# A sort that begins with a small first part, and layer ends without padding tiles and without edge counts

## The chip, the cores and the metric

The kernel runs on one core of a Trainium2 chip. The metric is the device time of one execution in microseconds (us), the median of several runs. A measurement of this kernel can tell about 0.2% (8 us) from no change.

## The reference, cut to what matters

There are 3125 nodes with 128 features and 103,125 directed edges (sorted by `dst`), each with one of nine types. `edge_index` is `[src, dst]`, so the sums of the first part run over `src`: the edges come in the wrong order for them.

```
# three layers (l = 0, 1, 2), 9 weight matrices 128x128 and 9 biases each
X = einsum('ne,ref->rnf', out, weights[l])
msg = X[edge_type, dst] + biases[l][edge_type]
hidden = segment_sum(msg, src, num_segments=N);  relu except after the last
x = layernorm(x + hidden)
# attention over the same edges
alpha = cos(x[row], x[col]) * beta, softmax over each row's edges
out = segment_sum(alpha * x[col], row)
x = layernorm(x + out)
```

## The kernel before, in words

The kernel has four stages.

**The sort (0 to 526 us).** The edges lie in SBUF as 128 rows of 808 columns. They have to be put in the order of their `src` group (31 groups of `RB` = 102 nodes, one more for padding: `NK` = 32 buckets). VectorE (DVE) makes the group number of each edge, then for each bucket a 0/1 map over all 808 columns (`eq`, L425). TensorE (PE) counts these maps (two products of 404 columns per bucket, L1067). From the counts DVE works out bucket totals (`counts`; PE spreads them, L1071), and the place of each bucket's first edge on each row (`bases`, L458). It also packs each edge into one word (`word`, L460 to L467). Then `place(lo, n, first)` works through all 32 buckets for `n` columns: PE makes the place of each edge by two products into one of two PSUM banks (`bucket`, L1078 and L1079), and DVE takes the maximum over buckets (L475, L479). The first `CP` = 332 columns are placed first; GpSimd (POOL) then scatters them, one indirect DMA per column, into a table in DRAM (L1036), which SyncE's queue (SP) loads back (L905). The other `EP` = 476 columns are placed next; they are not scattered but put in order by products of one-hot matrices on PE (L1148, 476 x 4), which end in PSUM. Both results are added; PE and DVE make the list of gathers from it (`rows`), which releases POOL's gathers.

Beside it PE makes layer 0's products x times weights (`first_x`, 75 steps of a bias product L1097 and a product L1099; each is copied by ScalarE (ACT), and stored by SP). Sixteen of them stand between the buckets of the 476 columns, one after every second bucket; the other 59 follow, and the one-hot products L1148 come behind all of them. The bias is split into three bf16 parts by POOL (L1021 to L1030), on 96 rows x 1152 columns, and POOL also writes the selection matrices (`choose`, L1015).

**Three layers (526 to 3619 us).** Each layer has `GT` = 806 gathers, one tile of 128 edges each, by POOL (L1054), into a ring of `GR` = 62 slots. PE multiplies each gathered tile by a one-hot matrix (`use_tiles`, L1193, four tiles to a PSUM bank), DVE adds the result to the group's sum (`take_tiles`, L665) and makes later one-hots (`one_hot`, L594). As a tile can belong to two groups, and to round up to turns of `BODY` = 24, a layer has `NT` = 840 tile places in 35 turns (`TURNS`); the gathers end at place 836 at the latest. Turns 0 to 83 of all 105 turns also count edges between nodes: 10 steps per turn with five 128x510 products each (L1202), whose one-hots DVE makes (L599, L600), and which ACT evicts at each group's end. Blocks 0 to 19 of the next layer's products x times weights are made early, inside the layer, and are stored by SP. At the layer's end the last six groups are turned (`turn_sums`, L1226), DVE takes the relu (L675), blocks 20 to 24 are made (L1237, DVE adds the bias, L689) and stored by five DMAs (L912); POOL's first gather of the next layer waits for these stores. Blocks 0 to 19 are then made again without stores, unless one came too early, and the next layer's tiles follow.

**The attention (3619 to 3999 us)** works on dense 128x384 blocks. The change doesn't touch it.

Of the kernel before, what the change touches and what calls it, by code (L numbers as in the profile page):

```python
# [47 lines left out]
def gnn_program(nc, x, src, dst, edge_type, weights, biases, beta, out):  # L48
# [32 lines left out]
    CP = 332  # L81
    EP = ET - CP
# [33 lines left out]
    AT_TURN = [-(-(REACH[k] * NT // MB + BODY) // BODY) for k in range(EARLY)]  # L116
    PAIR_BANKS, ALL_BANKS = (6, 7), (5, 6, 7)
    EARLY_STORES, ALL_STORES = EARLY + 1, 2 * EARLY + 1
# [14 lines left out]
    assert (L - 1) * TURNS < CTURNS < L * TURNS and CB % CR == 0 and CQ + CR < KW  # L133
# [23 lines left out]
    counts = nc.dram_tensor("edge_counts", (NB, P, NP), F32, kind="Internal").ap()  # L157
    absent = nc.dram_tensor("edge_absent", (NB, P, NP), BF16, kind="Internal").ap()

    with ExitStack() as ctx:  # L160
# [63 lines left out]
        bias_d = part(RF)  # L224
        bias_x = [part(RF // 2, BF16) for _ in range(3)]
# [20 lines left out]
        bias_t, ones_3 = bias[:, 0:RF // 2].bitcast(BF16), bias[:, RF // 2:RF // 2 + P // 2].bitcast(BF16)  # L246
# [47 lines left out]
        s_bias = sem("s_bias")  # L294
        s_eq = sem("s_eq")
# [60 lines left out]
        UNITS, CONSTANTS, BIAS_PARTS = 15, 21, 33  # L356
# [36 lines left out]
        def _(dve):  # L393
# [19 lines left out]
            nc_.memset(zerob[:, :], 0.0)  # L413
# [10 lines left out]
            for b in range(NK):  # L424
                nc_.tensor_scalar(eq[:, b, :], keyb, float(b), None, ALU.is_equal).then_inc(s_eq, 1)  # L425

# [33 lines left out]
            step(nc_.tensor_scalar(posi, posi, float(MB - 1), -float(RB), ALU.min, ALU.mult))  # L460
            step(nc_.tensor_tensor(posi, srci, posi, ALU.add))

            step(nc_.scalar_tensor_tensor(out=word, in0=dsti, scalar=float(R), in1=typei,
                                          op0=ALU.mult, op1=ALU.add))
            step(nc_.scalar_tensor_tensor(out=word, in0=posi, scalar=float(1 << ROW_BIT), in1=word,
                                          op0=ALU.mult, op1=ALU.add))
            step(nc_.tensor_scalar(word, word, 1.0, None, ALU.add))  # L467

# [15 lines left out]

            place(0, CP, 0)
            ti, tj = (t.bitcast(I32)[:, 0:CP] for t in tmps[0:2])
# [158 lines left out]
            for q in range(CR - 1):  # L645
                cell_hots(q)

            def take_tiles(l, i, cells):
                first = NT * l
                for u in range(BODY):  # L650
                    n, t = divmod(u, SLOTS)
                    if t == 0:
# [792 lines left out]
```

## Time and profile before

| | |
|---|---|
| median of 3 runs | 3996.73 us (3995.7 to 3997.86) |
| the profiled execution: its time, its span | 4001.13 us, 3999.4 us |
| busy: PE, DVE, POOL, ACT | 73%, 68%, 66%, 20% |
| POOL gathers: layers 1 and 2, layer 0 | 1612 and 806, 945 and 948 ns each |
| TensorE's granted clock, mean | 0.847 |

The profile shows one execution. A busy share is an average over four stages with different limits, so the stages are read one by one: the chain of waits tells which engine's work ends last, the timeline of each engine shows when its instructions start, how long they take and what ended the idle time before them, and the table by windows gives the granted clock of TensorE (1.00 is 2.4 GHz, 0.50 is 1.2 GHz).

### The profile page before, as it was taken

Reading aid. Unit: us, or ns where it says so; the run is one execution under the profiler, and the core shown is the slowest. Engines: PE = TensorE matmul, PEld = TensorE weight load, DVE = VectorE, ACT = ScalarE, POOL = GpSimd, SP = SyncE. Lnnn points to the kernel's source line nnn. Section 1 sums busy time; section 2 is a strip of 40 time slices with the busy share of each in tenths; the row PEclk is TensorE's granted clock in tenths of the full one; section 3 lists DMA queues with packets and bytes.
Section 4 is the critical chain, followed back from the end, with each engine's and each line's share of the span. In section 5 each row is a group of like instructions: output and inputs, shape, how many; then the busy total and the mean of one; then the engine's idle time right before and its main releaser. Section 6 shows DMA issues by size and latency. Waiting matters only on the chain.

```text
span 3999.4 us, 57212 instructions
## 1 busy us (share of the span) xinstructions
PE 2913.7 (73%) x14372; PEld 1860.7 (47%) x14372; DVE 2714.3 (68%) x9164; ACT 801.6 (20%) x1939; POOL 2632.2 (66%) x2787
## 2 busy tenths in 40 slices
PE   6999966676777678777777777787774444447998
PEld 2555544444444445444444444554443333335776
DVE  6488875676667668776767665777664333337999
ACT  0688801000100010100100010001000000004665
POOL 4777767777777775777777777577777777770000
PEclk6999988898889989998899888999885555557999
DMA  2300012342433332333343333323333111113554
GB/s 83 135 2 2 2 42 73 88 108 73 107 88 103 73 108 83 80 85 103 83 106 79 103 86 79 115 73 75 87 78 73 53 53 53 53 53 115 193 190 135
DMA packets 374776, 337.04 MB, mean 84 GB/s; under 512 B 262929, under 2 KB 326985, under 8 KB 374342
## 3 DMA queue, kind: packets, MB, share of 16 engines
q0 software_dynamic: 88000, 158.81, 16.4%
q1 hardware_dynamic: 83110, 113.84, 8.3%
q10 hardware_dynamic: 203360, 60.73, 6.2%
q8 instruction: 141, 2.31, 0.2%
q14 instruction: 165, 1.35, 0.1%
HBM read 226.02 MB, written 130.74 MB: 89 GB/s over the span
## 4 chain that ended last, share of the span: by engine, by line
POOL 46%; PE 26%; issue 17%; DVE 7%; DMA 3%; ACT 1%; SPq 0%; DVEq 0%; POOLq 0%; ACTq 0%
POOL region L1054 46%; PE ps L1148 9%; PE ps L1193 3%; PE ps L1276 3%; PE ps L1202 3%; PE ps L1237 3%; DMA region<-x_of_type_in_layer,arrays 2%; PE ps L1304 2%; PE ps L1099 1%; DVE region L792 1%; DVE region L665 1%; DVE region L599 1%; PE ps L1279 1%; DVE region L600 1%; PE ps L1079 1%
## 5 line engine op out<-in xcount | busy, mean ns | idle before, releaser
L1054 POOL DMA_INDIRECT region<-x_of_type_in_layer,arrays x1612 | 1523.3, 945 | 552.3 <-issue 477.9
L1193 PE MATMUL ps<-region,oh 128*102 x5040 | 1112.6, 324 | 789.9 <-SPq L918 490.4
L1193 PEld LDWEIGHTS ps<-region,oh 128*102 128x102 f32 x5040 | 920.9, 204 | 1340.6 <-issue 1078.6
L1202 PE MATMUL ps<-region 128*128 128x510 f16 x4200 | 1355.0, 410 | 182.6 <-ACT ps L1362 138.7
L594 DVE TENSOR_SCALAR oh<-iota_w,arrays 128x102 f32<-128x102 f32 x2528 | 730.1, 290 | 1051.6 <-PE ps L1193 1026.3
L1054 POOL DMA_INDIRECT region<-x_of_type,arrays x806 | 763.7, 948 | 265.5 <-issue 263.0
L665 DVE TENSOR_TENSOR region<-region,ps 102x128 f32 x2520 | 713.9, 283 | 3.1 <-issue 2.8
L1202 PEld LDWEIGHTS ps<-region 128*128 128x128 f16 x4200 | 433.6, 104 | 249.5 <-issue 197.8
L1373 ACT COPY region<-ps 128x510 f32<-128x510 f32 x155 | 89.8, 579 | 2246.4 <-PE ps L1202 2245.9
L599 DVE TENSOR_SCALAR region<-ps,arrays 128x640 f16<-128x640 f16 x844 | 459.6, 545 | 0.0
L1036 POOL DMA_INDIRECT scattered_edges<-region x332 | 322.4, 971 | 155.6 <-issue 106.3
L600 DVE TENSOR_SCALAR region<-ps,arrays 128x510 f16<-128x510 f16 x844 | 400.0, 474 | 0.0
L1148 PE MATMUL ps<-region 128*128 128x420 f16 x1904 | 340.6, 340 | 0.0
L1343 ACT ACTIVATE region<-region 128x128 f16<-128x128 f16 x952 | 291.8, 389 | 44.2 <-DVE region L572 43.9
L1148 PEld LDWEIGHTS ps<-region 128*128 128x128 f16 x1904 | 184.8, 97 | 156.1 <-issue 0.9
L573 DVE TENSOR_SCALAR region<-region 128x840 f16<-128x840 f16 x476 | 248.0, 521 | 0.0
L1237 PE MATMUL ps<-wsb,hB 128*128 128x384 f32 x540 | 210.5, 544 | 9.0 <-DVE hB L675 8.8
L689 DVE TENSOR_TENSOR region<-ps,bias 128x384 f32<-128x384 f32 x270 | 148.7, 551 | 64.6 <-PE ps L1237 61.9
L1304 PEld LDWEIGHTS ps<-nodes,region 128*128 128x128 f32 (+1 forms) x1250 | 163.8, 191 | 53.9 <-DVE region L792 28.5
L1304 PE MATMUL ps<-nodes,region 128*128 128x129 f32 (+1 forms) x1250 | 181.3, 282 | 7.2 <-DVE region L792 7.0
L572 DVE TENSOR_SCALAR region<-region 128x128 f16<-128x128 f16 x476 | 121.8, 256 | 82.3 <-PE ps L1148 82.1
L1276 PE MATMUL ps<-hB,region 128*128 128x384 f32 (+1 forms) x450 | 170.8, 461 | 0.0
(243 smaller groups left out, 1621.3 us busy)
## 6 DMA issues: line engine op xcount, KB each, us to landing
x_of_type_in_layer<-region SPq DMA_DIRECT2D x90, 576.0 KB
edge_counts<-region ACTq DMA_DIRECT2D x155, 255.0 KB
arrays<-edge_counts SPq DMA_DIRECT2D x40, 960.0 KB, 5.0
region<-x_of_type_in_layer,arrays POOLq DMA_INDIRECT x1612, 2.5
edge_absent<-region ACTq DMA_DIRECT2D x155, 127.5 KB
region<-edge_absent SPq DMA_DIRECT2D x40, 480.0 KB, 3.8
region<-x_of_type,arrays POOLq DMA_INDIRECT x806, 2.5
x_of_type<-x0st SPq DMA_DIRECT2D x51, 192.0 KB, 1.9
```

The costliest lines, as they stand in the source:

```text
L594: ins = nc_.tensor_scalar(oh[:, t % U, 0:RB], iota_r, rowf[:, t % NT:t % NT + 1], None, ALU.is_equal)
L599: nc_.tensor_scalar(cl[:, q % CR, :], lane_h, key1[:, q:q + 1], None, ALU.is_equal)
L600: nc_.tensor_scalar(cr[:, q % CR, :], lane_h[:, 0:CW], key2[:, q:q + 1], None, ALU.is_equal).then_inc(s_co, 1)
L665: nc_.tensor_tensor(h, h, ps[0:RB, 6 + n % 2, t * D:(t + 1) * D], ALU.add).then_inc(s_add, 1)
L1036: pool.indirect_dma_start(out=table, out_offset=bass.IndirectOffsetOnAxis(ap=pay[:, t, 1:2], axis=0), in_=pay[:, t, 0:1], in_offset=None). ...
L1054: pool.indirect_dma_start(out=grow[:, t % GR * D:(t % GR + 1) * D], out_offset=None, in_=xts[l], in_offset=bass.IndirectOffsetOnAxis(ap=gi ...
L1148: mm = pe.matmul(ps[:, 2 * d + n, 0:HW], oh_q[:, k, d, :], oh_s[:, k, n * HW:(n + 1) * HW], start=False, stop=False, skip_group_check=True)
L1193: mm = pe.matmul(ps[0:RB, 6 + n % 2, t * D:(t + 1) * D], oh[:, u % U, 0:RB], grow[:, bass.ds(at[u % PAIRS], D)], start=True, stop=True)
L1202: mm = pe.matmul(ps[:, c, 0:CW], cl[:, q % CR, c * P:(c + 1) * P], cr[:, q % CR, :], start=False, stop=False, skip_group_check=True)
L1237: pe.matmul(ps[:, banks[j % len(banks)], 0:G3], hB[:, b * P:(b + 1) * P], wsb[:, l * R + 3 * c:l * R + 3 * c + 3, :].rearrange("p r d -> p ...
L1304: mm = pe.matmul(ps[0:w, 4 + c % 2, t * VW:(t + 1) * VW], ring[:, b % RING, t * P:t * P + w], nodes[:, j, :], start=False, stop=(j == NB - ...
L1343: ins = act.activation(oh_q[:, k, d, :], hot_q[:, k, :], ACT.Copy, scale=cols[:, 4 * t + 2 + d:4 * t + 3 + d])
```

## The change

It has two parts. All times of day stay out here; the numbers are sizes.

**The sort.**
- A first part of `CA` = 64 columns is placed, and written out as `first_cells`, before the other 268 of the 332 (`cells`); POOL starts its scatters at `first_cells` and waits for `cells` at column 64. The buckets are worked through three times (64, 268, 476 columns).
- The packing of `word` moves from behind `bases` to behind the maps `eq`, ahead of the counts. The list of group ends (`late` to `past`) moves behind the last `place`.
- Of the 75 `first_x` steps, eight come before the buckets (two ahead of the totals' product, six behind it), one after every second bucket of the 268 and of the 476 columns (16 + 16), and 35 after.
- The bias is split by POOL on 9 rows x 128 columns (five short instructions in place of thirteen), goes to DRAM in three parts, and comes back as 3 rows x 1152. The other layers' biases are loaded behind it.
- `choose` is written by ACT, not by POOL.
- PE begins with 24 products of zeros (`WARM`), 512 columns each.
- POOL waits for layer 0's stores before it waits for `rows`.

**The layer ends.**
- Tile places 836 to 839 are left out in each layer (`LAST_USE`); the semaphores are advanced by as much.
- The last turn of each layer, and the first turn of layers 1 and 2, count no edges (`QUIET`); the 84 counting turns are now the others, 0 to 87.
- The first eight one-hots of a layer are made behind the products of blocks 20 to 24, not in the last turn of the layer before.
- Block 24 is stored in three pieces (`PIECES`).

```diff
@@ sort, DVE
             for b in range(NK):
                 nc_.tensor_scalar(eq[:, b, :], keyb, float(b), None, ALU.is_equal).then_inc(s_eq, 1)
+            step(nc_.tensor_scalar(posi, posi, float(MB - 1), -float(RB), ALU.min, ALU.mult))
...
+            step(nc_.tensor_scalar(word, word, 1.0, None, ALU.add))
...
-            place(0, CP, 0)
...
+            place(0, CA, 0)
+            cells(0, CA, "first_cells")
+            place(CA, CP - CA, NK)
+            cells(CA, CP, "cells")
+            place(CP, EP, 2 * NK)
...
-            place(CP, EP, NK)
             dve.wait_ge(s_fill, 16)
+            dve.wait_ge(s_later, 32)
@@ sort, POOL
-            finished(nc_.tensor_copy(choose[0:2 * NK, :, :],
-                                     chosen[0:2 * NK, :].unsqueeze(2).to_broadcast([2 * NK, NK, P])))
...
-            H3 = 3 * NK
-            finished(nc_.tensor_copy(bias_x[0][0:H3, :], bias[0:H3, 0:RF]))
...
+            finished(nc_.tensor_copy(bias_x[0][0:R, :], bias_s[0:R, :]))
...
-            pool.wait_ge(s_d, marks["cells"])
+            pool.wait_ge(s_d, marks["first_cells"])
             for t in range(CP):
+                if t == CA:
+                    pool.wait_ge(s_d, marks["cells"])
@@ sort, PE
+            pe.wait_ge(s_d, marks["zeros"])
+            for n in range(WARM):
+                pe.matmul(ps[:, 7, :], zerob[:, 0:P], zerob[:, :], start=True, stop=True)
...
+            pe.wait_ge(s_const, 64)
+            turn_nodes(0)
+            pe.wait_ge(s_parts, 64)
+            for q in range(2):
+                first_x(q)
+            pe.wait_ge(s_d, marks["counts"])
+            pe.matmul(ps[:, 0, 0:NK], ones[0:NK, :], tot_diag[0:NK, :], start=True, stop=True).then_inc(s_t, 1)
+            for q in range(2, FIRST_X):
+                first_x(q)
+            pe.wait_ge(s_d, marks["bases"])
+            pe.wait_ge(s_pool, CONSTANTS)
+            pe.wait_ge(s_choose, 1)
             for b in range(NK):
-                bucket(0, CP, b, b)
...
+                bucket(0, CA, b, b)
             for b in range(NK):
-                bucket(CP, EP, b, NK + b)
+                bucket(CA, CP - CA, b, NK + b)
                 if b % 2:
-                    first_x(b // 2)
-            for q in range(NK // 2, NB * XC):
+                    first_x(FIRST_X + b // 2)
+            for b in range(NK):
+                bucket(CP, EP, b, 2 * NK + b)
+                if b % 2:
+                    first_x(FIRST_X + NK // 2 + b // 2)
+            for q in range(FIRST_X + NK, NB * XC):
                 first_x(q)
@@ sort, SP
-            sp.dma_start(bias[:, :], biases.rearrange("l r f -> (l r f)").partition_broadcast(P)).then_inc(s_bias, 16)
+            sp.dma_start(bias_s[0:R, :], biases[0]).then_inc(s_bias, 16)
...
+            sp.wait_ge(s_pool, BIAS_PARTS)
+            for n in range(3):
+                sp.dma_start(bias_parts[n].rearrange("(r d) -> r d", r=R), bias_x[n][0:R, :]).then_inc(s_parts, 16)
+            sp.wait_ge(s_parts, 48)
+            sp.dma_start(bias_t, bias_parts).then_inc(s_parts, 16)
@@ layers
+    QUIET = {TURNS * l + i for l in range(L) for i in (0, TURNS - 1)} - {0}
+    CELLS_IN = [n for n in range(L * TURNS) if n not in QUIET]
+    LAST_USE = NT - SLOTS
...
+                for u in range(min(BODY, LAST_USE - i * BODY)):
...
-                    one_hot(first + i * BODY + u + U)
+                    if i * BODY + u + U < NT:
+                        one_hot(first + i * BODY + u + U)
...
                     take_made(l, LATE_BLOCKS, ALL_BANKS)
+                    for u in range(U):
+                        one_hot(NT * l + u)
...
+                types = R // PIECES[b]
+                for lo in range(0, R, types):
```

How the instructions stand, on the engines that wait or are waited for. PE at the program's start, before:

```order
L1060 UNCONDITIONAL_BRANCH
L1067 MATMUL ps<-region 64x404 x64
L1071 MATMUL ps<-region,ones 128x32
L1078 MATMUL ps<-region 128x332
L1079 MATMUL ps<-region 128x332
```

PE at the program's start, now (L1094 are the products of zeros, L1099 the counts, L1114 the transposes of the nodes, L1125 and L1127 a `first_x` step, L1137 the totals):

```order
L1089 UNCONDITIONAL_BRANCH
L1094 MATMUL ps<-zerob 128x512 x24
L1099 MATMUL ps<-region 64x404 x64
L1114 MATMUL ps<-ident,nodes 128x128 x8
L1125 MATMUL ps<-bias 128x384
L1127 MATMUL ps<-wsb,hB 128x384
L1125 MATMUL ps<-bias 128x384
L1127 MATMUL ps<-wsb,hB 128x384
L1137 MATMUL ps<-region,ones 128x32
```

Two `first_x` steps and the transposes for them stand ahead of the totals' product; six more steps follow it, and then the buckets of 64 columns.

DVE from `bases` (L458) to the end of the first `place`, before (L460 to L467 pack the words, L475 and L479 take the maximum over buckets):

```order
L458 CAST region<-region 64x808
L460 TENSOR_SCALAR arrays<-arrays 128x808
L461 ISA arrays<-arrays 128x1616
L463 SCALAR_TENSOR_TENSOR arrays<-arrays 128x808
L465 SCALAR_TENSOR_TENSOR arrays<-arrays 128x808
L467 TENSOR_SCALAR arrays<-arrays 128x808
L475 COPY arrays<-ps 128x332 x2
L479 TENSOR_TENSOR arrays<-arrays,ps 128x332 x30
L481 TENSOR_TENSOR arrays<-arrays 128x332
```

DVE from `bases` (L482) to `first_cells` (L505), now:

```order
L482 CAST region<-region 64x808
L490 COPY arrays<-ps 128x64 x2
L494 TENSOR_TENSOR arrays<-arrays,ps 128x64 x30
L496 TENSOR_TENSOR arrays<-arrays 128x64
L497 TENSOR_SCALAR arrays<-arrays 128x64
L502 TENSOR_SCALAR arrays<-arrays 128x64
L503 TENSOR_SCALAR arrays<-arrays 128x64
L504 COPY region<-arrays 128x64
L505 SCALAR_TENSOR_TENSOR region<-arrays 128x64
L490 COPY arrays<-ps 128x268 x2
```

The packing is gone from here, and the first part is 64 columns wide and complete before the 268 begin.

PE at the end of layer 0, before (L1193 a tile, L1202 counts of edges, L1226 `turn_sums`, L1237 `make_x`):

```order
L1193 ISA
L1193 MATMUL ps<-region,oh 102x128
L1202 MATMUL ps<-region 128x510 x2
L1193 ISA
L1193 MATMUL ps<-region,oh 102x128
L1202 MATMUL ps<-region 128x510 x2
L1226 MATMUL ps<-ident,region 128x102 x6
L1237 MATMUL ps<-wsb,hB 128x384 x15
L1226 MATMUL ps<-ident,region 128x102 x25
```

PE at the end of layer 0, now (L1234 a tile, L1267 `turn_sums`, L1278 `make_x`):

```order
L1234 ISA
L1234 MATMUL ps<-region,oh 102x128
L1234 ISA
L1234 MATMUL ps<-region,oh 102x128
L1267 MATMUL ps<-ident,region 128x102 x6
L1278 MATMUL ps<-wsb,hB 128x384 x15
L1267 MATMUL ps<-ident,region 128x102 x25
```

The counts of edges between the tiles are gone from this turn, and it is four tiles shorter.

## Rows read from the trace of the kernel before

**Rows 1.** The page, part 4: shares of the chain that ended last, by line.
```profile
POOL region L1054 46%; PE ps L1148 9%; PE ps L1193 3%; PE ps L1276 3%; PE ps L1202 3%; PE ps L1237 3%; DMA region<-x_of_type_in_layer,arrays 2%; PE ps L1304 2%; PE ps L1099 1%; DVE region L792 1%; DVE region L665 1%; DVE region L599 1%; PE ps L1279 1%; DVE region L600 1%; PE ps L1079 1%
```

**Rows 2.** Windows: length; busy (count) PE, PEld, DVE, ACT, POOL; clock, DMA.
```profile
16.00:19.00 3.00, 1.88 (x8) 0.71 (x6) 3.00 (x2) 0.00 (x0) 2.94 (x2) 1.00 0.97 258
...
28.00:31.00 3.00, 3.00 (x12) 1.63 (x11) 3.00 (x11) 0.00 (x0) 0.08 (x1) 0.61 0.00 0
...
90.00:95.00 5.00, 5.00 (x15) 1.58 (x15) 2.33 (x5) 0.96 (x2) 3.78 (x5) 0.82 0.14 46
```

**Rows 3.** Timeline of DVE in the sort: start, us, instruction [idle before, releaser].
```profile
13.10 19.40 DVE L425 TENSOR_SCALAR region<-arrays 128x808 bf16<-128x808 bf16 x32
35.74 0.57 DVE L431 COPY region<-ps 64x404 f32<-64x404 f32 x1 [3.25 <-PE ps L1067]
...
45.11 0.58 DVE L460 TENSOR_SCALAR arrays<-arrays 128x808 int32<-128x808 int32 x1
...
49.44 0.91 DVE L475 COPY arrays<-ps 128x332 f32<-128x332 f32 x2
...
52.45 0.50 DVE L479 TENSOR_TENSOR arrays<-arrays,ps 128x332 f32<-128x332 f32 x1 [0.28 <-PE ps L1079]
...
75.94 0.50 DVE L490 SCALAR_TENSOR_TENSOR region<-arrays 128x332 int32<-128x332 int32 x1
...
84.83 0.65 DVE L479 TENSOR_TENSOR arrays<-arrays,ps 128x476 f32<-128x476 f32 x1 [1.97 <-PE ps L1079]
85.85 0.65 DVE L479 TENSOR_TENSOR arrays<-arrays,ps 128x476 f32<-128x476 f32 x1 [0.37 <-PE ps L1079]
...
96.10 1.26 DVE L479 TENSOR_TENSOR arrays<-arrays,ps 128x476 f32<-128x476 f32 x2 [0.77 <-PE ps L1079]
```

**Rows 4.** Timeline of PE in the sort: a product of `first_x`.
```profile
120.41 0.81 PE L1099 MATMUL ps<-wsb,hB 128*128 128x384 f32 x2
```

**Rows 5.** Timeline of POOL in the sort: its first scatter.
```profile
77.36 1.22 POOL L1036 DMA_INDIRECT scattered_edges<-region  x1 [49.28 <-DVE shiftcol L496]
```

**Rows 6.** Timeline of SP's queue: the load of the scattered table.
```profile
507.27 0.32 SPq L905 DMA_DIRECT2D arrays<-scattered_edges  x1
```

**Rows 7.** Chain that ended last, in order of time: start, us, what.
```profile
166.22 1.67 PE ps L1119 x4
...
172.69 340.36 PE ps L1148 x1904
...
524.41 0.50 POOLq L362
```

**Rows 8.** Timeline of PE at the ends of layer 0 and layer 2.
```profile
1537.23 0.46 PE L1193 MATMUL ps<-region,oh 128*102 x2 [2.11 <-SPq L918]
...
1545.57 1.03 PE L1226 MATMUL ps<-ident,region 102*128 102x102 f32 x6 [2.90 <-DVE region L665]
...
3613.01 3.73 PE L1193 MATMUL ps<-region,oh 128*102 x16 [3.30 <-SPq L918]
3618.75 5.50 PE L1226 MATMUL ps<-ident,region 102*128 102x102 f32 x31 [2.01 <-issue]
```

**Rows 9.** Timeline of DVE at layer 0's end: the last bias sums.
```profile
1558.68 1.78 DVE L689 TENSOR_TENSOR region<-ps,bias 128x384 f32<-128x384 f32 x3 [0.16 <-PE ps L1237]
```

**Rows 10.** Timeline of POOL at the layer ends, and 62 gathers later.
```profile
1534.25 0.96 POOL L1054 DMA_INDIRECT region<-x_of_type,arrays  x1 [0.30 <-issue]
1564.01 0.94 POOL L1054 DMA_INDIRECT region<-x_of_type_in_layer,arrays  x1 [28.80 <-DMA x_of_type_in_layer<-region]
...
1641.16 0.94 POOL L1054 DMA_INDIRECT region<-x_of_type_in_layer,arrays  x1 [2.54 <-PE ps L1193]
...
2678.18 0.94 POOL L1054 DMA_INDIRECT region<-x_of_type_in_layer,arrays  x1 [1.80 <-PE ps L1193]
```

**Rows 11.** The page, part 6: a DMA of 192 KB, us to landing.
```profile
x_of_type<-x0st SPq DMA_DIRECT2D x51, 192.0 KB, 1.9
```

**Rows 12.** Windows at layer 0's end, columns as in rows 2.
```profile
1552.00:1553.00 1.00, 1.00 (x4) 0.56 (x3) 0.21 (x2) 0.00 (x0) 0.00 (x0) 0.65 0.15 65
```

More of the change, by code:

```diff
@@ L223, in gnn_program @@
         twice, chosen, tot_diag = part(NK), part(NK), part(NK)
-        bias_d = part(RF)
-        bias_x = [part(RF // 2, BF16) for _ in range(3)]
+        bias_s, bias_d = part(D), part(D)
+        bias_x = [part(D // 2, BF16) for _ in range(3)]
         used[0] = MB * D
@@ L412, in _ @@
             step(nc_.memset(typei[:, REST:ET], 0), "cleared")
-            nc_.memset(zerob[:, :], 0.0)
+            step(nc_.memset(zerob[:, :], 0.0), "zeros")
             nc_.memset(nodes[:, :, D:VW], 1.0)
@@ L646, in _, with take_tiles @@
                 cell_hots(q)
-            def take_tiles(l, i, cells):
-                first = NT * l
-                for u in range(BODY):
+            def take_tiles(l, i):
+                first, cells = NT * l, CELLS_IN.get(TURNS * l + i)
+                for u in range(min(BODY, LAST_USE - i * BODY)):
                     n, t = divmod(u, SLOTS)
@@ L1069, in _ @@
             mm.then_inc(s_t, 1)
-            pe.wait_ge(s_d, marks["counts"])
-            pe.matmul(ps[:, 0, 0:NK], ones[0:NK, :], tot_diag[0:NK, :], start=True, stop=True).then_inc(s_t, 1)
             def bucket(lo, n, b, k):
-                if b == 0:
-                    pe.wait_ge(s_d, marks["bases"])
                 if k >= 2:
@@ L1179, in _, with use_tiles @@
                       skip_group_check=True)
-            def use_tiles(l, i, cells):
-                first = NT * l
-                for u in range(BODY):
+            def use_tiles(l, i):
+                first, cells = NT * l, CELLS_IN.get(TURNS * l + i)
+                for u in range(min(BODY, LAST_USE - i * BODY)):
                     n, t = divmod(u, SLOTS)
@@ L1186, in use_tiles @@
                         at, due = steps_at((i * BODY + u) // PAIRS)
-                    if cells and u == 0:
-                        ready = banks_at(TURNS * l + i)
+                    if cells is not None and u == 0:
+                        ready = banks_at(cells)
                     if t == 0:
@@ L1195, in use_tiles @@
                     if t == SLOTS - 1:
-                        mm.then_inc(s_used, 1)
-                    for q, c in PARTS[u] if cells else ():
-                        k = i * CB + (CB * TURNS * l + q)
+                        mm.then_inc(s_used, 1 if i * BODY + u < LAST_USE - 1 else 1 + (NT - LAST_USE) // SLOTS)
+                    for q, c in PARTS[u] if cells is not None else ():
+                        k = cells * CB + q
                         if c == 0:
@@ L1256, in _ @@
                         pe.wait_ge(s_xe, made[0])
[L1257 removed]
+                    use_tiles(l, i)
             pe.wait_ge(s_cz, CG + CG * MB)
@@ L1326, in copy_turned @@
                 act.copy(hB[:, 4 * c * P:(4 * c + n) * P], ps[:, 2 + c % 2, 0:n * P]).then_inc(s_x0c, 1)
+            act.wait_ge(s_pool, CONSTANTS - 2)
+            act.copy(choose[0:2 * NK, :, :],
+                     chosen[0:2 * NK, :].unsqueeze(2).to_broadcast([2 * NK, NK, P])).then_inc(s_choose, 1)
             copy_turned(0)
```

115 lines of the change are left out of this document (60 added, 55 removed).

## The prediction

> **What bounds the kernel now.** I read the chain of waits first: POOL's gathers hold 46% of it, PE's one-hot products of the sort 9% [rows 1]. Layer by layer the gathers follow each other without gaps, apart from the stretch between two layers (28.8 us of idle time at the first [rows 10]) and one stall 62 gathers later. So three stretches are worth something: the sort ahead of the first gather, the ends of the layers, and these stalls. Work that PE or DVE loses inside a layer is worth nothing, since POOL's 806 gathers end it.
>
> In the sort two paths meet. POOL's scatters start at 77.36 [rows 5] and end in SP's load at 507.27 [rows 6]. PE's 1904 one-hot products start at 172.69 and end at 172.69 + 340.36 = 513.05 [rows 7]. The load needs about 1.9 us (a smaller one does [rows 11]), so POOL's path has up to 513.05 - 507.27 - 1.9 = 3.9 us of slack. Both paths must get shorter, or nothing is won.
>
> **The sort, as far as the first scatter.** The 32 maps `eq` take DVE 19.4 us, from 13.10 to 32.50 [rows 3]. Their pace is not even: 2 instructions touch the window 16 to 19, in which POOL is busy for 2.94 us with splitting the bias, and 11 the window 28 to 31, in which POOL is idle [rows 2]. I read 0.28 us for one without POOL. The change leaves POOL five instructions on 128 columns, on a bias that lands early, and gives `choose` to ACT; so I take 32 x 0.28 = 9.0 us, and the maps end at 22.1. (The Trainium skill, "SBUF — State Buffer", section "Who interferes with whom", says that VectorE in a 2-port mode and GpSimd lock a shared port pair, and that the later one fully blocks. The rows agree; without that lock the maps would stay at 32.5, which is a rival below.)
>
> Now the packing of words follows, which stood between 45.11 and the first COPY at 49.44 [rows 3], 4.3 us: 26.4. PE's 64 products for the counts must be done too: 12 of them touch the window 28 to 31 at a clock of 0.61 [rows 2], 0.25 us each, and by the clock 0.15 at 1.00. From the first map at 13.4 on that ends between 23.2 and 29.4. I take 27.0 for the first copy of the counts, before 35.74 [rows 3]. The 24 products of zeros matter only here, for 0 to 3 us. (The Trainium skill, "TensorE: Matmul & The Clock Gate", section "What's actually happening", has the slow clock as the state at rest. The row of 16 to 19 shows 1.00 before any long activity [rows 2], so here the trace differs. By the page the counts would start slowly without the zeros; by the row they start fast anyway. The sum goes by the 27.0.)
>
> From there to `bases` nothing changes: 45.11 - 35.74 = 9.4 us, 36.4. Meanwhile PE has eight `first_x` steps at 0.81 [rows 4], 6.5 us, in two gaps that are idle now; if they ran at the slow clock (about 1.55, below) they would delay `bases` or the buckets by up to 4 us. SP gets two new waits here: for POOL's split, and for the parts in DRAM. Behind them stand the load of the parts (which PE's first step needs), the other biases, and the fill of the table (which POOL's first scatter needs). The loads kept the DMA engines busy at 16 to 19 and had drained by 28 to 31 [rows 2]; now the first of them is 9 rows in place of 128, so the two trips to DRAM, 1.9 us each [rows 11], end before PE asks for the parts near 28. I cost this at nothing; if the loads drain no earlier, the totals, and with them everything, come up to 4 us later.
>
> The first part then has 32 buckets of 64 columns. A bucket of 332 columns took 0.50 + 0.28 = 0.78 us [rows 3]. For 64 columns this is the upper end, 0.25 (a DVE instruction that short) the lower. What is left is the way from PE to DVE and back, over two banks; I take 0.36, near the lower end. 36.4 + 0.4 + 32 x 0.36 + 1.3 for six short instructions = 49.6, before 75.94 + 0.50 = 76.44 [rows 3]. **POOL's scatters start 26.8 us earlier**, at 50.5, if the 0.9 us from the mark to the start stay [rows 3, 5]. The second 268 columns are wanted 64 scatters (about 80 us) later and are ready by then.
>
> **The sort, PE's path.** From 48.2 on PE has 16 pairs of buckets (268 columns) with a `first_x` each, 16 pairs of 476 columns, 35 more `first_x`, and the close. The price depends on the clock. A pair of 476 with its step took 0.65 + 1.97 + 0.65 + 0.37 = 3.64 us at 0.5, and 1.26 + 0.77 = 2.03 at 1.00 [rows 3]; in between the clock rose at about 91.8 [rows 2], some 15 us after pairs and steps had begun. At the fast clock the buckets of a pair are 2.03 - 0.81 = 1.22; with 268 columns between 0.69 (by width) and 1.22, and I take 0.9: 1.7 for the pair with its step. At the slow clock a bucket of 332 is 0.78, of 268 about 0.67, and a step 3.64 - 2 x 1.05 = 1.55: 2.9 for the pair. The buckets of 64 leave PE mostly idle, so I expect the slow clock at 48.2 and, as before, a rise after some 15 us: 5 pairs x 2.9 + 11 x 1.7 = 33.2, to 81.4. Then 16 x 2.03 = 32.5, to 113.9; 35 x 0.81 and some transposes = 29.3, to 143.2; the close as before, 172.69 - 166.22 = 6.5 [rows 7], to 149.7. **PE's path is 23.0 us shorter.** DVE's list of group ends, now behind the last `place` (3 us), lies beside the 35 steps; POOL's path, 26.8 shorter and with slack, is not the bound. POOL also does its load of a value (0.50 [rows 7]) and six waits ahead of `rows`: 0 to 1.3 us, I put 0.5.
>
> **The layer ends.** After the last gather PE had eight tiles with counts of edges, from 1537.23 until DVE's sums let it turn them at 1545.57: 8.3 us [rows 8]. Now it has four tiles without counts. Layer 2's end shows tiles without counts: eight took 3.73, and 3618.75 - 3613.01 - 3.73 = 2.0 more went by for DVE's sums and one-hots [rows 8]. Four tiles: 2.0, and 1.0 for four sums without one-hots. Gain 8.3 - 3.0 = 5.3 (4.3 if the 2.0 stay, 6.3 if the clock is high). The last store: from the last bias sum at 1558.68 + 1.78 = 1560.46 to POOL at 1564.01 were 3.55 us [rows 9, 10]; with a last piece of 192 KB 1.9 [rows 11] + 0.9 = 2.8: 0.8 less (0 to 1.6). The eight one-hots stand behind all of this. 6.1 per boundary, 12.2 for both.
>
> The stalls at 1641.16 and 2678.18 were ended by PE's tiles [rows 10]: 2.54 + 1.80, less the usual 0.30 each, 3.7 us. The first turn without counts gives PE and DVE 24 tiles' worth of lead before the ring is full, more than the 1.7 us that the moved one-hots take, so I take the whole 3.7 (0 if the turns behind it fall back). At the end of layer 2 four tiles fewer give 5.7 - 3.0 = 2.7.
>
> **Sum.** 23.0 + 0.5 + 12.2 + 3.7 + 2.7 = 42.1 us. The profiled execution took 4001.1: 3959.0; it lies 4.4 above the median of the runs, so 3954.6, say **3955**.
>
> **The rivals.**
> - *POOL becomes the sort's bound.* If the clock rises soon after 48.2, the first pairs cost 16 x 1.7 = 27 and PE gains 29; POOL's path allows 26.8 + 3.9. For it: at layer 0's end the clock rose faster, some 7 us after PE began to turn the sums at 1545.57 [rows 8, 12]. 6 us more: 3949. Chance 0.20.
> - *The clock stays low through the 268 columns.* 16 x 2.9 = 46.4, then 4 pairs x 3.64 + 12 x 2.03 = 39: PE's products start near 169, the sort gains 3.3, in all 22: 3974. For it: before, the whole first `place` went at 0.78 a bucket, that is at the slow clock, and nothing raised it. Chance 0.15.
> - *The maps don't get faster* (the change doesn't do what I read into it, the slow ones being DVE's own): maps and words end at 36.8, everything is 9.8 later, 3965. Against it: the two windows [rows 2]. Chance 0.05.
> - *The layer ends give it back*: the turn without counts lets the clock fall, and the 15 products between layers run longer at 1.55 in place of 0.81. They already start slow (0.65 in the window in which it rises [rows 12]); some 5 us lost at each boundary, and the stalls stay: 3966. Chance 0.08.
> - *Slower:* the clock stays low until the `first_x` are done. Then 46.4 + 16 x 3.64 + 35 x 1.55 + 0.9 + 6.5 = 166 from 48.2 on: the products start at 214, 42 us later than now, and the other gains of 19 leave 22 us lost: 4019. It decides itself at about 157 us: a clock that rises before that leaves the kernel no slower. Against it: it rose at 92 in the same mix. Chance 0.05, of which a good half ends within 0.2% of before or near it.
>
> **How the numbers follow.** The forecast has 0.47. The range 3944 to 3975 takes in the quick clock with two or three us more at the ends, and the late clock; what it leaves out is the slow case and part of the tails. 0.2% is 8 us, about what a measurement of this kernel can tell: faster 0.95, same 0.03, slower 0.02.
>
> **What would show it.** Right: `eq` at 0.28 each; the first scatter near 50; the one-hot products starting near 150 with the load of the table landed before they end; gaps of about 24 us between layers; no POOL stall 62 gathers into layers 1 and 2. Wrong: a granted clock of 0.5 well past 75, a wait of PE for the bias parts ahead of the totals, or a first scatter later than 56.

## The result

The changed kernel is **slower**: a median of 4035.42 us against 3997.59 us before, 20 executions each. The ratio with its 95% interval, 1.0077 (1.0064 to 1.0089), leaves out as slow runs the four executions that lie over 1.5% above the fastest one; the ratio of the medians is 1.0095. The forecast was 3955 with a range of 3944 to 3975. The profiled execution took 4035.99 us with a span of 4034.2 us, 34.8 us more than the 3999.4 before. One of the 20 executions took only 3976.61 us, 48 us less than the next; its mean granted clock is 0.858, and that of the other 19 is 0.840 to 0.846. No trace of it was kept. What follows describes the others.

Three rows divide this. The lines of POOL's gathers and PE's one-hot products after (line, engine, operation, count: shortest/median/longest in ns, first and last start in us; forms):

```profile
L1189 PE MATMUL ps<-region x1904: 338/341/559, 223.8 to 564.8; 128*128 128x420 f16 x191
L1083 POOL DMA_INDIRECT region<-x_of_type,arrays x806: 940/944/1428, 577.5 to 1585.7; - x162
L1083 POOL DMA_INDIRECT region<-x_of_type_in_layer,arrays x1612: 940/944/1048, 1610.5 to 3646.6; - x180
```

The one-hot products start at 223.8, before at 172.69 [rows 7], and the first gather at 577.5 where it was 526.2: the sort lost 51.3 us. From the first gather to the last go 3069.1 us, before 3083.7: the layers gained 14.6. Behind the last gather the span needs 387.6 in place of 389.5: another 1.9 gained. 51.3 - 14.6 - 1.9 = 34.8. So the layer ends did what they were to do, and the whole loss lies ahead of the first gather.

**The granted clock tells where.** The table by windows of the kernel after, with the busy time and the number of instructions of each engine, then the granted clock, the DMA share and GB/s:

```profile
20.00:30.00 10.00, 8.26 (x38) 3.99 (x36) 9.59 (x19) 2.03 (x4) 0.00 (x0) 0.94 0.65 206
30.00:40.00 10.00, 10.00 (x17) 3.11 (x16) 3.85 (x15) 2.39 (x5) 0.00 (x0) 0.50 0.27 98
...
90.00:100.00 10.00, 10.00 (x22) 3.44 (x23) 2.60 (x6) 1.43 (x3) 7.56 (x9) 0.50 0.20 65
...
180.00:190.00 10.00, 10.00 (x23) 3.95 (x24) 10.00 (x33) 3.47 (x8) 7.56 (x9) 0.71 0.32 108
190.00:200.00 10.00, 10.00 (x29) 3.59 (x28) 2.77 (x9) 4.34 (x10) 6.54 (x7) 1.00 0.50 169
```

PE is busy for at least 9.9 of the 10 us of every slice from 30 on, and yet it has the 1.2 GHz level until about 185; before, the clock was back at about 92 [rows 2]. It came back 18 us after the last bucket had ended (at 167.5), when only `first_x` steps were left.

**The second thing is the price of a step.** The timeline of PE, once at a clock of 0.50 and, from 200 on, once at 1.00 (start, busy time, line, operation, rows and columns of the two operands):

```profile
150.62 0.49 PE L1125 MATMUL ps<-bias 3*128 3x384 bf16 x1
151.04 1.65 PE L1127 MATMUL ps<-wsb,hB 128*128 128x384 f32 x2
152.48 0.61 PE L1106 MATMUL ps<-region 128*128 128x476 bf16 x1
...
200.59 0.33 PE L1125 MATMUL ps<-bias 3*128 3x384 bf16 x1
200.86 0.91 PE L1127 MATMUL ps<-wsb,hB 128*128 128x384 f32 x2
201.70 0.33 PE L1125 MATMUL ps<-bias 3*128 3x384 bf16 x1
```

At 1.00 a step takes 201.70 - 200.59 = 1.11 us; before it took 0.81 [rows 4]. The operands are the same but for one: the bias product has 3 rows (3x384) where it had 96. The list of the change said so ("3 rows x 1152"), and the working priced only the trip of these rows through DRAM, not the product. At 0.50 a step takes 152.48 - 150.62 = 1.86 within a pair, some 0.3 more than the forecast's 1.55, and 2.01 where only steps are left.

**What the price is** stands in the loads of weights, which have an engine row of their own (PEld). In the kernel before, with 96 rows, they run beside the product ahead:

```profile
121.06 0.35 PEld L1099 LDWEIGHTS ps<-wsb,hB 128*128 128x128 f32 x2 [0.23 <-issue]
121.54 0.10 PEld L1097 LDWEIGHTS ps<-bias 96*128 96x128 bf16 x1
```

There the f32 product starts at 121.22 and the next bias product at 121.86, so that both loads are early. The same stretch of the kernel after:

```profile
200.59 0.09 PEld L1125 LDWEIGHTS ps<-bias 3*128 3x128 bf16 x1 [0.55 <-issue]
200.85 0.30 PEld L1127 LDWEIGHTS ps<-wsb,hB 128*128 128x128 f32 x2 [0.17 <-issue]
201.70 0.09 PEld L1125 LDWEIGHTS ps<-bias 3*128 3x128 bf16 x1 [0.55 <-ACT x0st L1378]
201.96 0.19 PEld L1127 LDWEIGHTS ps<-wsb,hB 128*128 128x128 f32 x1 [0.17 <-issue]
```

Each load starts when its own product does (200.59 beside 200.59, 201.96 0.26 behind the bias product's 201.70): it has not started beside the product ahead. The bias load's 0.09 and the first f32 load's 0.19 are 0.28 of the 0.30 us.

### The profile page after: what moved, and what is told of

It is laid out like the page before. It is cut to its first block, busy times and chain, and to the rows that moved or that the text cites. A ratio compares the mean times of both kernels' runs of the same rounds, so it can differ in the third digit from the quotient of the medians.

```text
span 4034.2 us, 57356 instructions
## 1 busy us (share of the span) xinstructions
PE 2993.4 (74%) x14434; PEld 1869.5 (46%) x14436; DVE 2695.3 (67%) x9182; ACT 803.5 (20%) x1940; POOL 2617.6 (65%) x2780
## 4 chain that ended last, share of the span: by engine, by line
POOL 41%; PE 29%; issue 15%; DVE 9%; DMA 3%; ACT 2%; DVEq 0%; SPq 0%; POOLq 0%; ACTq 0%
POOL region L1083 41%; PE ps L1189 8%; PE ps L1243 4%; PE ps L1234 4%; PE ps L1316 3%; DMA region<-x_of_type_in_layer,arrays 2%; PE ps L1127 2%; PE ps L1344 2%; DVE region L687 2%; DVE region L620 2%; PE ps L1278 2%; DVE region L621 1%; DVE region L816 1%; PE ps L1107 1%; DVE oh L615 1%
## 5 line engine op out<-in xcount | busy, mean ns | idle before, releaser
L1234 PE MATMUL ps<-region,oh 128*102 x5016 | 1102.4, 322 | 779.6 <-SPq L952 477.1
L1234 PEld LDWEIGHTS ps<-region,oh 128*102 128x102 f32 x5016 | 911.1, 202 | 1337.7 <-issue 1078.2
L594 DVE TENSOR_SCALAR region<-region 128x840 f16<-128x840 f16 x476 | 238.6, 501 | 0.0
L1278 PE MATMUL ps<-wsb,hB 128*128 128x384 f32 x540 | 212.5, 548 | 9.4 <-DVE hB L698 8.5
```

Source lines behind the costliest of these rows:

```text
L1234: mm = pe.matmul(ps[0:RB, 6 + n % 2, t * D:(t + 1) * D], oh[:, u % U, 0:RB], grow[:, bass.ds(at[u % PAIRS], D)], start=True, stop=True)
L1278: pe.matmul(ps[:, banks[j % len(banks)], 0:G3], hB[:, b * P:(b + 1) * P], wsb[:, l * R + 3 * c:l * R + 3 * c + 3, :].rearrange("p r d -> p ...
```

## The experiments

**1. The layer ends alone.** The kernel before with the lines marked "layers" of the diff; the sort untouched.

> The kernel before with the layer-end half of the change alone (the quiet first and last turns, the last uses left out, the block that is stored in three pieces); the sort is that of before. First theory, that the two halves are independent and the loss lies in the sort alone: the stretch from the first gather to the last shortens by 14 to 15 us and the end behind the last gather by about 2, as in the changed kernel, so some 16 us less than before: about 3981. Rival, that the layer ends gained only because the sort was late (more of the counts' work had to wait): under 8 us gained, 3990 or more.

Measured 3983.26 us, ratio 0.9961 (0.9946 to 0.9976). POOL's timeline at the first boundary:

```profile
1556.37 0.94 POOL L1068 DMA_INDIRECT region<-x_of_type_in_layer,arrays  x1 [23.22 <-DMA x_of_type_in_layer<-region]
```

The idle time is 23.22 us (28.8 before [rows 10]); the second boundary has 25.70. From the first gather to the last go 3070.3 us, 13.4 less than before, and the end is 2.7 shorter. This half is worth about 16 us by the trace and 14.5 by the medians, with the sort of before as with the changed one, and the rival is out. (The profiled span is 18.3 shorter; 2.2 of that are a first gather that came earlier by itself.)

**2. The row count of the bias product alone, in the order of before.** One line of the kernel before, with 32 and then with 64 rows:

```diff
-                pe.matmul(ps[:, 4 + q % 4, 0:G3], ones_3[0:3 * NK, :], bias_t[0:3 * NK, c * G3:(c + 1) * G3],
+                pe.matmul(ps[:, 4 + q % 4, 0:G3], ones_3[0:NK, :], bias_t[0:NK, c * G3:(c + 1) * G3],
```

> The kernel before with one thing changed: the bias product of each of the 75 steps of the first X runs over 32 rows instead of 96 (it leaves out the two smaller parts of the bias in layer 0, nothing else). First theory, the row count of the bias product is what makes a step dear and also what holds the clock down: a step alone takes about 1.1 us fast and 2.0 slow (0.81 and 1.57 before), the clock, which rose at about 92 in the kernel before, rises only after the 32 pairs of 476 columns, near 150, and PE starts the one-hot products at 212 or later instead of 172.7: 4037 or more. Second theory, the price is real but the clock goes by the order of the work alone: the clock rises at about 92 as before, 75 x 0.29 = 22 us are lost, start near 195, about 4020. Third theory, 32 rows cost nothing more than 96 (three rows were dear for another reason, or the step was dear through its neighbours): the time of before, 3997.

> The kernel before with the bias product on 64 rows instead of 96 (it leaves out the smallest part of the bias in layer 0, nothing else). If any row count of 64 or less that stands next to 128 costs the change: a step alone 1.1 us fast as with 32 rows, the clock late again, 4037 or more. If the price grows with the rows that are missing: about halfway between 96 and 32 rows, 0.95 us fast, 4015 to 4025. If 64 is as free as 96: 3997.

Measured 4048.27 us, ratio 1.0123 (1.0106 to 1.014), with 32 rows, and 4043.65, ratio 1.0114 (1.0097 to 1.0132), with 64: this one line loses more than the whole change. A step alone takes 1.11 us at 1.00 with either, here the 32-row kernel:

```profile
180.59 0.33 PE L1097 MATMUL ps<-bias 32*128 32x384 bf16 x1
...
181.70 0.33 PE L1097 MATMUL ps<-bias 32*128 32x384 bf16 x1
```

So next to 128 rows 3, 32 and 64 cost the same, and 96 cost nothing extra: it is not the number of rows that is paid, but the change from one class to another. Between two products of 64 rows the load is early again. In the 64-row kernel, where the bias product follows a bucket's second product, it lies beside the bucket's product (from 112.07 on) and ahead of its own (at 112.45), and nothing waited for it:

```profile
112.08 0.11 PEld L1097 LDWEIGHTS ps<-bias 64*128 64x128 bf16 x1
```

Three rows behind 64 are a change again. In the changed kernel, also at 0.50, the bias load starts with its own product (at 150.62), and that product starts 0.51 us behind the bucket's 64-row product, where it was 0.38 above; 32 rows behind 64 give the same 0.51:

```profile
150.61 0.10 PEld L1125 LDWEIGHTS ps<-bias 3*128 3x128 bf16 x1 [0.41 <-issue]
```

The rows tried thus fall into three classes: 3 and 32, 64, and 96 and 128.

The clock, too, follows. In the windows of the 32-row kernel it is at 0.50 until 140 although the order of the work is that of before:

```profile
90.00:100.00 10.00, 10.00 (x18) 2.59 (x18) 2.65 (x5) 1.44 (x3) 7.56 (x9) 0.50 0.13 41
...
140.00:150.00 10.00, 10.00 (x29) 3.82 (x28) 10.00 (x34) 4.17 (x10) 7.56 (x9) 0.91 0.40 138
```

The one-hot products start at 211.8 (32 rows) and 215.0 (64). The second theory (195) is out: the narrow first part is not needed for the low clock. (The Trainium skill, "TensorEngine Tiling (Array Packing)", lists in its section "Available Configurations" modes of 128, 64 and 32 rows, and its section "Key Properties" says that changing the mode drains TensorE. The runs agree if a product is taken to run in the smallest mode that holds its rows, which no run shows directly: 64 rows or fewer next to 128 pay, 32 or 3 next to 64 pay, 96 next to 128 do not.)

**3. The changed kernel with 96 rows again.** The three rows of bias stay where they are; 93 rows of zeros, written by DVE while it waits for the edges, go below them.

```diff
-        bias_t, ones_3 = bias[0:3, 0:RF // 2].bitcast(BF16), bias[0:3, RF // 2:RF // 2 + P // 2].bitcast(BF16)
+        bias_t, ones_3 = bias[0:96, 0:RF // 2].bitcast(BF16), bias[0:96, RF // 2:RF // 2 + P // 2].bitcast(BF16)
...
+            step(nc_.memset(bias_t, 0.0), "bias_zero")
...
-            sp.dma_start(bias_t, bias_parts).then_inc(s_parts, 16)
+            sp.wait_ge(s_d, marks["bias_zero"])
+            sp.dma_start(bias_t[0:3, :], bias_parts).then_inc(s_parts, 16)
```

> The changed kernel with the bias product on 96 rows again (the three rows of bias with 93 rows of zeros below them), all else as changed. First theory, the three rows make the steps dear and hold the clock down: a step alone costs 0.81 fast and 1.57 slow again, the clock rises within the part of 268 columns, PE starts the one-hot products near 150 instead of 224: about 3961. Second theory, only the price comes from the rows and the clock stays low until 185 because narrow buckets come first: about 64 x 0.44 + 11 x 0.29 = 31 us come back, start near 193, about 4004. Third theory, the rows are not it at all: start 224, 4035.

Measured **3959.49 us, ratio 0.9896 (0.988 to 0.9913)**: 76 us less than the changed kernel, and faster than before. PE's one-hot products in this kernel, and its windows:

```profile
L1191 PE MATMUL ps<-region x1904: 337/340/559, 150.5 to 490.8; 128*128 128x420 f16 x191
```

```profile
50.00:60.00 10.00, 10.00 (x26) 3.79 (x26) 3.23 (x8) 1.64 (x4) 7.56 (x9) 0.50 0.20 64
60.00:70.00 10.00, 10.00 (x39) 4.57 (x37) 3.84 (x10) 2.97 (x6) 7.56 (x9) 0.84 0.29 97
70.00:80.00 10.00, 10.00 (x43) 4.45 (x42) 5.09 (x13) 2.77 (x7) 7.56 (x9) 1.00 0.35 119
```

They start at 150.5 (the forecast had 149.7), the clock is back at about 63, some 17 us after the pairs of 268 columns began at 46.6 (the forecast had 15 us), and the first scatter starts at 49.1 (50.5). Stage by stage, from the starts of PE's products in the two traces:

| us | as changed, 3 rows | 96 rows |
|---|---|---|
| first bucket of 64 | 39.9 | 35.5 |
| 268 columns, 16 pairs with steps | 51.4 to 104.2 | 46.6 to 81.1 |
| 476 columns, 16 pairs with steps | 104.2 to 167.5 | 81.1 to 113.9 |
| 35 steps | to 216.2 | to 143.8 |
| close, to the first one-hot product | 223.8 | 150.5 |

The difference of 73.3 us is price and clock together. Price: at a clock of 0.50, 32 steps in pairs at 0.3 us each and some 15 outside of them at 0.45, and at 1.00 the other 28 at 0.30: 25 us by this estimate. The other 48 are put down to the clock, as what is left.

**4. The buckets' second product on 96 rows too.** It has 64 rows in both kernels, and in the changed one it stands next to 128 rows 96 times. `choose` and `base_h` get 32 rows of zeros:

```diff
+            nc_.memset(choose[2 * NK:96, :, :], 0.0)
+            nc_.memset(base_h[2 * NK:96, :], 0.0)
...
-                pe.matmul(ps[:, b % 2, 0:n], choose[0:2 * NK, b, :], base_h[0:2 * NK, lo:lo + n],
+                pe.matmul(ps[:, b % 2, 0:n], choose[0:96, b, :], base_h[0:96, lo:lo + n],
```

> The kernel of a_bias96 with the second product of each bucket (the one that adds a bucket's start) on 96 rows too, 32 of them zeros, instead of 64. First theory, any change of row class between neighbouring products costs about 0.1 us and holds the clock down: on top of a_bias96 the 96 buckets save 0.1 us each, 10 us, and the clock comes back sooner: start near 140 or earlier, 3951 or less. Second theory, only three rows are dear and 64 are not: the time of a_bias96 within 3 us.

> The changed kernel with only the second product of each bucket on 96 rows; the bias product keeps its 3 rows. By the price alone 96 x 0.1 = 10 us come back: start near 214, about 4025. If the clock goes by how many row changes a stretch holds, the part of 268 columns keeps the two changes of each step but loses the eight of its buckets, and the clock rises inside it: start 160 to 180, 3970 to 3990. If the clock goes by the 3-row products themselves, it stays low to the end of the buckets: 4025.

With both products on 96 rows: **3948.06 us, ratio 0.9869 (0.9852 to 0.9885)**, the fastest of the study. With the buckets alone, and the bias left on its 3 rows: 3968.42, ratio 0.9927 (0.991 to 0.9944). The price shows at equal clock (1.00) in PE's timeline, first with 64 and then with 96 rows, from one bias product to the next:

```profile
101.19 0.34 PE L1127 MATMUL ps<-bias 96*128 96x384 bf16 x1
...
102.01 0.36 PE L1108 MATMUL ps<-region 128*128 128x476 bf16 x1
102.30 0.37 PE L1109 MATMUL ps<-region 64*128 64x476 f16 x1
102.61 0.37 PE L1108 MATMUL ps<-region 128*128 128x476 bf16 x1
102.91 0.37 PE L1109 MATMUL ps<-region 64*128 64x476 f16 x1
103.22 0.34 PE L1127 MATMUL ps<-bias 96*128 96x384 bf16 x1
```

```profile
80.81 0.32 PE L1129 MATMUL ps<-bias 96*128 96x384 bf16 x1
...
81.61 0.36 PE L1110 MATMUL ps<-region 128*128 128x476 bf16 x1
81.81 0.37 PE L1111 MATMUL ps<-region 96*128 96x476 f16 x1
82.02 0.37 PE L1110 MATMUL ps<-region 128*128 128x476 bf16 x1
82.22 0.36 PE L1111 MATMUL ps<-region 96*128 96x476 f16 x1
82.43 0.32 PE L1129 MATMUL ps<-bias 96*128 96x384 bf16 x1
```

2.03 against 1.62 us: four changes of rows less, 0.10 us each. The products start 0.30 apart with changes and 0.20 without, while the busy time of one reads 0.36 to 0.37 in both: it is the distance of the starts that shows the price, not the duration. And the loads tell why, first with 64 rows, then with 96:

```profile
102.60 0.10 PEld L1108 LDWEIGHTS ps<-region 128*128 128x128 bf16 x1 [0.21 <-issue]
102.91 0.09 PEld L1109 LDWEIGHTS ps<-region 64*128 64x128 f16 x1 [0.21 <-issue]
```

```profile
82.02 0.10 PEld L1111 LDWEIGHTS ps<-region 96*128 96x128 f16 x1
82.22 0.10 PEld L1129 LDWEIGHTS ps<-bias 96*128 96x128 bf16 x1
```

With 64 rows a load starts with its own product (102.91 and 102.91), with 96 one product earlier (82.02 for the product at 82.22). The 0.10 us of a change are the load that nothing hides. My expectation of 0.1 per bucket was half of it, since a bucket has two changes.

With the bias on 3 rows and the buckets on 96, the clock was back near 52 and the products started at 153.3. So the 3-row products do not hold the clock down by themselves: in the order of the changed kernel it came back early without either kind of change, and only with both kinds it stayed away. (In this trace it had been up once already, from about 35.6 to 42.4, beginning among the 3-row steps ahead of the buckets; in the changed kernel's profile the same steps ended at 0.50.) With both on 96 rows PE's products run from 132.3 to 473.1, and POOL's last scatter starts at 475.2, so that POOL's path ends last: DVE waits 4.82 us for the table that SP loads back, and about 5 us of PE's gain are not seen. (The load took 2.86 us; the prediction had taken 1.9 for it from a smaller one.) That is the first rival of the prediction, in a kernel that it was not written for.

**5. Half as many changes, the same products.** The steps of the changed kernel in pairs: two bias products of 3 rows, then two of 128 (the edit is shortened).

```diff
-                pe.matmul(ps[:, 4 + q % 4, 0:G3], ones_3, bias_t[:, c * G3:(c + 1) * G3],
-                          start=True, stop=False)
-                pe.matmul(ps[:, 4 + q % 4, 0:G3], hB[:, b * P:(b + 1) * P], ...
+                for q in steps: pe.matmul(ps[:, 4 + q % 4, 0:G3], ones_3, ...
+                for q in steps: pe.matmul(ps[:, 4 + q % 4, 0:G3], hB[:, b * P:(b + 1) * P], ...
```

> The changed kernel with the steps of the first X in pairs: two bias products of 3 rows, then the two steps of 128 rows, so 38 groups instead of 75 with the same products. If the price hangs on each change of rows, half of it goes: 37 x 0.4 = 15 us, start near 209, 4020, and less if the clock comes back sooner. If every 3-row product is dear by itself, nothing changes: start 224, 4035.

Measured 3979.59 us, ratio 0.995 (0.9932 to 0.9968), 56 us less than the changed kernel, with every product on its old rows. PE's timeline at 1.00 (two bias products, then the two steps of two products each):

```profile
141.66 0.49 PE L1126 MATMUL ps<-bias 3*128 3x384 bf16 x2
...
143.57 0.49 PE L1126 MATMUL ps<-bias 3*128 3x384 bf16 x2
```

143.57 - 141.66 = 1.91 us for two steps, that is 2 x 0.81 + 0.29: one price for two. The price hangs on the change. And the clock was at 1.00 from 60 on, so here as well fewer changes brought it back; that was worth more than the 15 us of price.

**6. The clock raised by force.** The changed kernel with 32 products of 404 columns on 128 rows between the narrow buckets and the 268 columns:

```diff
+            for n in range(NK):
+                pe.matmul(ps[:, 2, 0:HALF_ET], ltri_up[:, :], eq[:, n, 0:HALF_ET], start=True, stop=True)
```

> The changed kernel with 32 products of 404 columns (128 rows, results unused) put on PE between the narrow buckets and the part of 268 columns; nothing is left out. First theory, products that change between 3, 64 and 128 rows hold the clock down: it rises during the dense stretch and falls to 0.50 again in the part of 268 columns, the added products cost up to 32 x 0.34 = 11 us at the slow clock, start of the one-hot products 224 to 235, 4035 to 4046. Rival, the clock was low only because of the wait and the narrow buckets ahead, and stays up once it is up: pairs with a step of about 1.9 and 2.3 us, start near 173, about 3984.

Measured 3983.28 us, ratio 0.9958 (0.9943 to 0.9973): 52 us less than the changed kernel, for 7.6 us of products that nobody reads. The windows:

```profile
40.00:50.00 10.00, 10.00 (x57) 5.76 (x58) 6.20 (x28) 0.00 (x0) 0.00 (x0) 0.50 0.05 20
50.00:60.00 10.00, 10.00 (x42) 4.68 (x42) 2.28 (x10) 0.44 (x1) 6.00 (x6) 0.79 0.02 2
60.00:70.00 10.00, 10.00 (x41) 4.29 (x40) 4.37 (x11) 3.02 (x7) 7.56 (x9) 1.00 0.30 100
...
150.00:160.00 10.00, 10.00 (x28) 3.50 (x27) 0.00 (x0) 4.35 (x10) 7.66 (x8) 1.00 0.51 177
```

**My theory falls in one point here.** I expected the clock to fall back among the row changes; it stayed at 1.00 from 60 to 160, with 3, 64 and 128 rows in turn, and the products started at 173.0, which was the rival's number. So the changes did not pull a fast clock down here. What the runs show is narrower: buckets and steps that start slow and both change rows stayed slow as long as the buckets lasted (three kernels: as changed, and with 32 and 64 rows of bias in the old order), and the clock came back 18, 8 and 6 us behind the last bucket, among the steps alone. In the order of the changed kernel the same work came up within 17 us of the first pair once one kind of change was gone, halved, or preceded by products without changes. And it is a tendency: the one execution of 3976.61 us of the changed kernel is as fast as the kernels in which the clock came back early.

**7. Does it hold in the old order, too?** The edit of experiment 4 in the kernel before, and the same with the layer ends of experiment 1.

> The kernel before with the second product of each bucket on 96 rows instead of 64, nothing else. If a change of rows is dear and keeps a low clock low in any order of the sort: each of the 64 buckets saves its two changes, about 0.2 us, and the clock, low from 41 to 91 in the kernel before, comes back inside the part of 332 columns; the first scatter starts at 60 to 70 instead of 77, PE's one-hot products at 150 to 160 instead of 172.7, and since POOL's scatters would then end last, some 10 to 17 us are gained: 3980 to 3988. If it is dear only together with the narrow buckets: 3997.

> The kernel of h_before_choose96 with the layer-end half of the change on top. The layer ends do not meet the sort, so 16 us less than h_before_choose96: 3964 to 3972. What separates it from ae_both96 (3948) is then what the small first part and the products between the buckets are worth by themselves once no product changes rows: about 20 us.

Measured 3985.58 us, ratio 0.9973 (0.9963 to 0.9982), and 3969.63, ratio 0.9935 (0.9918 to 0.9951). The clock of the first was at 0.85 in 50 to 60, where the kernel before has 0.50; PE's products started at 153.5 in place of 172.7, the first scatter at 66.6 in place of 77.36. (4.6 us of the scatter's 10.8, and some of the products' 19, are not the edit's: PE's counts ended at 27.3 in place of 35.6, at a clock of 1.00 in the window 20 to 30; the 32-row kernel of experiment 2 had its counts as early, and lost all the same.) POOL's last scatter starts at 494.1 and PE's last product at 494.0, so that 19 us of PE's path bring the first gather only 16 forward. The rows cost something in both orders. And h2_ends_choose96 against ae_both96, 3969.63 against 3948.06, is what the changed sort is worth where neither the buckets nor the steps change rows: about 22 us.

## Why the prediction was wrong

**The step that failed** is in "The sort, PE's path", where a step was taken at 0.81 and 1.55 us and a pair of 268 columns at 2.9 and 1.7, all from rows of the kernel before. Those rows had a bias product of 96 rows. With 3 rows a step is 1.11 and 2.01, and the pair of 268 with its step took 3.24 at the slow clock. The sentence after it, "as before, a rise after some 15 us", fell with it: the clock stayed at 0.50 until 185, 134 us after the pairs had begun. With the one line put back to 96 rows, the rest of that paragraph holds: 34.5 us for the 268 columns (33.2 forecast), 32.8 for the 476 (32.5), 29.9 for the 35 steps (29.3), 6.7 for the close (6.5), the products at 150.5 (149.7), the kernel at 3959 (3955).

**The slower rival** had the right event, a clock that stays low until the `first_x` are nearly done, and the products at 214; they started at 223.8: the pairs began 3.2 us later than it had them and took 11.4 us longer, mostly the price of the changes, while the 35 steps took 6.4 us less, since the clock rose at 185. It had a chance of 0.05, because the prediction saw nothing that would keep the clock from rising: "it rose at 92 in the same mix". It was not the same mix. Before, only the buckets' 64-row products made changes; now the steps between them do as well.

**As far as the first scatter** the forecast was right but for one term. DVE's timeline after:

```profile
11.23 9.36 DVE L440 TENSOR_SCALAR region<-arrays 128x808 bf16<-128x808 bf16 x32
...
24.84 0.57 DVE L455 COPY region<-ps 64x404 f32<-64x404 f32 x1
...
40.39 0.49 DVE L490 COPY arrays<-ps 128x64 f32<-128x64 f32 x2 [6.22 <-PE ps L1107]
41.11 0.56 DVE L494 TENSOR_TENSOR arrays<-arrays,ps 128x64 f32<-128x64 f32 x2 [0.23 <-PE ps L1107]
41.82 0.55 DVE L494 TENSOR_TENSOR arrays<-arrays,ps 128x64 f32<-128x64 f32 x2 [0.16 <-PE ps L1107]
```

The maps took 9.36 us (9.0 forecast; 19.4 before [rows 3]) with POOL busy for 1.11 us of their time and a DMA share of 0.81 to 0.93, so POOL's work was what had slowed them, and not the loads. They also began at 11.23, where the forecast kept the 13.10 of before. The counts' first copy came at 24.84 (27.0), and `bases` was written by 34.17 (36.4). Two buckets go every 0.71 us, 0.36 each as forecast. But DVE waits 6.22 us for PE ahead of them: the six steps behind the totals, costed at nothing as lying in idle gaps, ran mostly at the slow clock, and at the price of the row changes, until 39.9. The bound of "up to 4 us" was passed. The scatters started at 53.88 (50.5), which mattered little: POOL's last one started at 484.1, well ahead of PE's last product at 564.8.

**The layer ends** were right. POOL's timeline at the end of layer 0:

```profile
1585.67 0.95 POOL L1083 DMA_INDIRECT region<-x_of_type,arrays  x1 [0.30 <-issue]
1610.48 0.94 POOL L1083 DMA_INDIRECT region<-x_of_type_in_layer,arrays  x1 [23.86 <-DMA x_of_type_in_layer<-region]
```

The idle time is 23.86 us at this boundary and 23.93 at the next, about 5 less each than before (6.1 forecast); both stalls of [rows 10] are gone (3.7 forecast); the end is 1.9 shorter (2.7). In all 16.5 of the 18.6 that were forecast for these terms, and experiment 1 shows the same apart from the sort. The rival that the layer ends give it back is out. (By its own terms, 5 us at each boundary and the 3.7 of the stalls, it should have read 3968 and not 3966.)

## What to carry to other kernels

Before pricing a product by a row of the trace, compare its operands row for row with those of the new one: fewer rows move less data and can still cost more time, here a load of weights that nothing hides (0.10 us for bf16, 0.19 for f32, at the fast clock) at each change between the classes of 3 or 32, of 64, and of 96 or 128 rows. Pad such a product with rows of zeros past 64 where it stands in a stream of 128-row products, or put products of one class together; the padding was worth 74 us of the sort in the changed kernel. A forecast that lets the clock rise "as before" needs the same stream as before, not only the same amount of work.

## What was new about the hardware

- The price of a row change does not depend on how few the rows are (1.11 us a step with 3, 32 and 64 rows, 0.81 with 96). It is paid between 64 and 3 or 32 rows as well, not between 96 and 128 or 64 and 64, and it is seen in the distance between starts and in the loads' row, not in a product's busy time: 0.33 us for the bias product with 3 rows, and 0.32 to 0.34 with 96.
- TensorE was busy for at least 9.9 of every 10 us of its records and stayed at 1.2 GHz for 150 us (30 to 180 in the changed kernel), and 7.6 us of other products ahead of the same buckets and steps lifted it for all of them. **Left open** is what in the changes keeps a slow clock slow, the pauses for the loads or something in the products themselves: no run here had the pauses without the changes. Their mere count is not it: a pair of buckets with its step has four in the kernel before, where the clock rose, and four with 64 rows of bias, where it did not; there one of the loads left bare is the f32 one. What made the clock fall ahead of this was not tried; every kernel had a stretch of 0.50 to 0.65 somewhere between 30 and 50. With 3 rows of bias it fell at 29 to 30, among the six steps behind the totals, in all four profiles; with 96 rows it fell at 29 in one and was back by 33 (experiment 3), and held through these steps in the other (both products on 96).
